# Second mixture of experts: from computing every expert on every token to dispatching rows into capacity buffers by indirect DMA

## The chip, the cores and the metric

The kernel runs on one core of one Trainium2 chip. A core has TensorE (PE: matrix multiplies into PSUM), VectorE (DVE), ScalarE (ACT), GpSimd (POOL) and SyncE (SP, which here only issues DMAs). The engines run their own instruction lists and meet at semaphores. The metric is the device time of one execution in microseconds (us), as the median of several; lower is better. A trace of one execution shows when each instruction ran.

## The reference

Two layers on 8 x 512 = 4096 tokens of width 128. What the change touches is the second layer's mixture and what feeds it.

```python
x = x + s * g                       # end of layer 0: attention output s, gate g = silu(mixture of 64 experts)
xn = layernorm(x)
s = L1_attn(xn)                     # gates from xn, a scan over the 512 tokens of each batch row, a norm
# second mixture: 8 experts, each token picks 2, each expert takes at most 1281 rows
N, K, E = 4096, 2, 8
capacity = int(1.25 * N * K / E) + 1                  # 1281
k_probs, k_idx = top_k(softmax(xf @ router_w.T), K)   # k_probs normalised to sum 1
rank = running count of each expert over the (token, choice) pairs
keep = rank < capacity
buf[flat_e, slot] += xf[token_id] (kept ones)         # [8, 1281, 128]
h = silu(buf @ w1)                                    # w1: [8, 128, 512]
out_buf = h @ w2                                      # w2: [8, 512, 128]
combined = sum over the 2 choices of k_probs * out_buf[flat_e, slot] (kept ones)
g = silu(combined + xn)
x = x + s * g
```

## The kernel before

There are two phases with a barrier between them. `attention_phase` does the first layer's attention in eight stages of four steps (`tau`) each, and stores its results to DRAM. `mixture_phase` does the rest, and is what the change is about.

**Turns and units.** `run_stages` goes over two layers, in each over 8 turns of 512 tokens (`Turn(layer, i, p)`), in each turn over `NQ` = 33 units (layer 0: 64 experts of 64 hidden columns, two to a unit, and a shared expert) or 32 units (layer 1: 8 experts of 512 hidden columns, four units to an expert, `UPC`). Every expert is computed on every token; a gate of zero takes out what was not chosen. A unit is the same chain in both layers, on tiles of 128 x 512:

- PE: three float16 matmuls `m_h` (high and low halves of weight and input), L1510 to L1512
- ACT: Silu in place in PSUM, L1414
- DVE: times the gate row, `m_hid`, L1605
- ACT: high float16 half, `m_hidh`, L1408
- POOL: low half, `m_hidl`, L1375
- PE: three float16 matmuls into `m_y` (`down`), L1490 to L1492, four units later (`LAG`); for layer 1 two further ones per turn add the residual.

**Gates.** The gate rows come from DRAM, spread over partitions by DMAs of SP (`load_gate_pair`, `load_gates`), into a ring of four slots.

**What follows a turn.** While a turn's units run, each engine slips in steps of the turn before (`follow(b, q)` after unit `q`; the tables `PE_AT`, `ACT_AT`, `DVE_AT`, `POOL_AT` say at which). For layer 0 these are: silu of the mixture, times s, transposed, added (`xnew`), stored; layer norm (POOL does the inverse root `rstd`, L1384); transpose; router logits, the two best experts, their shares; the four recurrent gates (float32 matmuls L1559), the scan, a second norm (POOL `crstd`, L1394), the result `s1`; the running rank of each expert ("rank", "cut"), and the gate rows of layer 1 (`cwT`). POOL also splits the normed input in two halves (`m_oh`, `m_ol`, L1389, L1391). For layer 1 only silu, product, transposes and the add follow. The steps of layer 0's last turn run under layer 1's first turn.

**Order.** Each engine's list is fixed by this program; a wait on one engine holds all that is behind it there. The loops for POOL, PE and ACT are in registers (`passes`), those for SP and DVE partly written out.

## Time and profile before

| | |
|---|---|
| median of 3 runs | 1306.46 us (1305.22 to 1307.92) |
| the profiled execution | 1305.83 us, its span in the trace 1304.1 us |
| attention | 0 to about 514 us |
| first mixture's units (layer 0) | about 514 to 942 us |
| second mixture's units (layer 1) and the end | about 942 to 1304 us |
| busy share of the span | PE 92%, DVE 74%, ACT 72%, POOL 63% |

Times in the trace are microseconds from the start of the span. The profiled execution is 1.7 us longer than its span. Durations of one instruction are in ns where marked so; matmuls and activations overlap their neighbours by some tens to 160 ns, so the distance between two starts tells the pace and not the duration.

### The profile page before, as it was taken

What the parts mean: (1) busy time and instruction counts of PE and PEld (TensorE: products, weight loads), DVE (VectorE), ACT (ScalarE), POOL (GpSimd) and SP (SyncE); (2) the same over time, 40 slices, a digit from 0 to 9 for tenths busy, and PEclk for the clock granted to TensorE, in tenths of its full rate; (3) what the DMA queues carried; (4) which work ended last, traced back from release to release, by engine and by line L of the source; (5) the groups of instructions that cost most, each with busy time, mean ns of one, the idle gap of its engine ahead of it and who ended that gap; (6) DMA issues with size and microseconds to landing.
All of it is one profiled execution on the core that took longest, in us unless ns stands there. A gap on an engine that the chain in (4) does not pass through costs nothing.

```text
span 1304.1 us, 21815 instructions
## 1 busy us (share of the span) xinstructions
PE 1199.2 (92%) x5840; PEld 490.8 (38%) x5840; DVE 961.7 (74%) x1802; ACT 935.7 (72%) x1724; POOL 816.9 (63%) x769
## 2 busy tenths in 40 slices
PE   4689998989989996889999899999999999999998
PEld 3123333333333221334444344444444444444443
DVE  4798999989899995567788487777767555555554
ACT  1157676766767775778787577877878888888886
POOL 5423323323332123778888588878878888888887
PEclk9999999999999998999999899999999999999999
DMA  3323040412304037998989789999832333223310
GB/s 71 56 46 70 18 78 13 83 36 51 68 17 73 10 92 218 219 213 185 209 183 190 161 169 197 179 195 197 177 100 62 85 74 81 63 75 72 81 41 9
DMA packets 102171, 137.51 MB, mean 105 GB/s; under 512 B 15546, under 2 KB 54396, under 8 KB 101628
## 3 DMA queue, kind: packets, MB, share of 16 engines
q1 hardware_dynamic: 101532, 136.31, 48.7%
q8 instruction: 36, 0.59, 0.2%
q10 hardware_dynamic: 544, 0.13, 0.2%
q14 instruction: 59, 0.48, 0.1%
HBM read 116.09 MB, written 20.05 MB: 104 GB/s over the span
## 4 chain that ended last, share of the span: by engine, by line
PE 21%; issue 18%; POOL 14%; DMA 3%; ACT 2%; DVE 1%; POOLq 1%; SPq 0%; ACTq 0%; DVEq 0%
POOL m_hidl L1375 13%; DMA p_gates<-t_cw 3%; PE m_h L1510 3%; PE m_y L1490 3%; PE m_h L1512 3%; PE m_h L1511 3%; PE m_y L1492 3%; PE m_y L1491 3%; PE m_m L1559 1%; ACT m_hidh L1408 1%; DVE m_hid L1605 1%; SPq L159 0%; POOL m_rstd L1384 0%; ACT m_h L1414 0%; POOL m_oh L1389 0%
## 5 line engine op out<-in xcount | busy, mean ns | idle before, releaser
L1375 POOL TENSOR_TENSOR m_hidl<-m_hid,m_hidh 128x512 f16<-128x512 f32 x520 | 612.3, 1187 | 135.7 <-ACT m_hidh L1408 101.7
L1605 DVE TENSOR_TENSOR m_hid<-m_h,p_gates 128x512 f32<-128x512 f32 x512 | 348.8, 688 | 243.7 <-ACT m_h L1414 223.8
L707 ACT ACTIVATE a_probs<-a_score 128x512 f32<-128x512 f32 x512 | 293.0, 597 | 123.3 <-PE a_score L788 116.6
L1408 ACT ACTIVATE m_hidh<-m_hid 128x512 f16<-128x512 f32 x520 | 323.0, 621 | 75.9 <-DVE m_hid L1605 73.6
L1414 ACT ACTIVATE m_h<-m_h 128x512 f32<-128x512 f32 x520 | 302.1, 581 | 79.4 <-PE m_h L1512 71.1
L885 DVE TENSOR_REDUCE a_mx<-a_mxps 128x2 f32<-128x1024 f32 x256 | 306.3, 1213 | 38.2 <-PE a_mxps L779 37.5
L800 PE MATMUL a_ops<-a_probs,a_vst 128*32 128x512 f32 x1024 | 136.4, 605 | 0.8 <-ACT a_probs L707 0.8
L583 POOL TENSOR_TENSOR a_crstd<-a_cvareps,a_neghalf 128x1 f32<-128x1 f32 x32 | 18.6, 581 | 157.5 <-DVE a_cvareps L924 143.6
L1490 PE MATMUL m_y<-m_hidh,p_wdh 128*128 128x512 f16 (+1 forms) x264 | 101.0, 383 | 7.2 <-POOL m_hidl L1375 4.2
L788 PE MATMUL a_score<-a_qstack,a_kstack 128*128 128x512 f16 x256 | 96.9, 384 | 8.6 <-ACT a_probs L707 7.0
L788 PE MATMUL a_score<-p_gates,p_raw 128*128 128x512 f16 x256 | 98.8, 387 | 5.9 <-ACT a_probs L707 4.4
L1492 PE MATMUL m_y<-m_hidl,p_wdh 128*128 128x512 f16 (+1 forms) x264 | 100.8, 382 | 0.0
L1491 PE MATMUL m_y<-m_hidh,p_wdl 128*128 128x512 f16 (+1 forms) x264 | 100.8, 382 | 0.0
L779 PE MATMUL a_mxps<-p_raw,p_gates 126*128 126x512 f16 x256 | 83.4, 410 | 18.2 <-DVE a_mx L885 10.5
L1490 PE MATMUL m_y<-m_hidh,m_wdh 128*128 128x512 f16 x256 | 97.1, 379 | 1.3 <-POOL m_hidl L1375 1.3
L1492 PE MATMUL m_y<-m_hidl,m_wdh 128*128 128x512 f16 x256 | 97.0, 379 | 0.0
L1491 PE MATMUL m_y<-m_hidh,m_wdl 128*128 128x512 f16 x256 | 97.0, 379 | 0.0
L575 POOL TENSOR_TENSOR a_ctx<-a_oT,a_rden 128x128 f32<-128x128 f32 x32 | 14.1, 439 | 120.8 <-DVE a_rden L909 120.8
L779 PE MATMUL a_mxps<-a_kstack,a_qstack 126*128 126x512 f16 x256 | 76.5, 380 | 6.5 <-DVE a_mx L885 6.5
L1510 PE MATMUL m_h<-p_xh,p_wuh 128*128 128x512 f16 x132 | 51.9, 394 | 12.2 <-DVE m_hid L1605 9.3
L788 PEld LDWEIGHTS a_score<-a_qstack,a_kstack 128*128 128x128 f16 x256 | 24.1, 97 | 103.1 <-ACT a_probs L707 92.0
L788 PEld LDWEIGHTS a_score<-p_gates,p_raw 128*128 128x128 f16 x256 | 24.9, 97 | 99.6 <-ACT a_probs L707 87.4
(219 smaller groups left out, 1786.9 us busy)
## 6 DMA issues: line engine op xcount, KB each, us to landing
p_gates<-t_cw SPq DMA_DIRECT2D x256, 256.0 KB, 7.2
p_gates<-t_cw SPq DMA_DIRECT2D x32, 512.0 KB, 5.2
t_qparts<-a_qparts SPq DMA_DIRECT2D x32, 128.0 KB
p_raw<-up SPq DMA_DIRECT2D x8, 512.0 KB, 5.5
p_raw<-down SPq DMA_DIRECT2D x8, 512.0 KB, 6.3
m_sT<-t_s SPq DMA_DIRECT2D x16, 256.0 KB, 5.7
a_xin<-x SPq DMA_DIRECT2D x8, 256.0 KB, 3.5
t_kparts<-a_kparts SPq DMA_DIRECT2D x16, 128.0 KB
```

The source lines that it names most:

```text
L707: act.activation(probs[:, kt % 2, g, :], score[:, g % 2, :], ACT.Exp, scale=SCALE / (QS * QS)).then_inc(exp_done, 1)
L779: op = pe.matmul(mxps[:, j % 2, k, :], stack[0][where.p][0:ZROWS, qt, g, at, :], stack[1][where.p][0:ZROWS, :, g, at, :], start=True, stop ...
L788: pe.matmul(score[:, g % 2, :], stack[1][s.p][:, kt, g, tau, :], stack[0][s.p][:, :, g, tau, :], start=True, stop=True).then_inc(score_ful ...
L800: op = pe.matmul(ops[GT * g:GT * g + GT, :], vst[half][:, tau * NG + g, kt, :], probs[:, kt % 2, g, :], start=(kt == 0), stop=(kt == KT - ...
L885: dve.tensor_reduce(mx[ahead % 2][:, j // 2, g:g + 2], mxps[:, j % 2, :, :], AX.X, ALU.max).then_inc(mx_done, 1)
L1375: pool.tensor_tensor(hidl[0:r0, k % r, :], hid[0:r0, k % r, :], hidh[0:r0, k % r, :], ALU.subtract).then_inc(lo_done, 1)
L1408: act.activation(hidh[0:r0, k % r, :], hid[0:r0, k % r, :], ACT.Copy).then_inc(hi_done, 1)
L1414: act.activation(h, h, ACT.Silu, scale=1.0 / WS).then_inc(silu_done, 1)
L1490: pe.matmul(yps[:], wdh[n][0:r0, q, :], hidh[0:r0, r, :], start=(q == 0 and not n), stop=False)
L1491: pe.matmul(yps[:], wdl[n][0:r0, q, :], hidh[0:r0, r, :], start=False, stop=False)
L1492: pe.matmul(yps[:], wdh[n][0:r0, q, :], hidl[0:r0, r, :], start=False, stop=(q == NQ[n] - 1)).then_inc(dn_done, 1)
L1605: dve.tensor_tensor(hid[:, k % r, :], hps[:, k % HBANKS[s.layer], :], gates[:, (q // UPC[s.layer]) % (SLOTS * GROUP), :], ALU.mult).then_i ...
```

## The change

Layer 1 leaves `run_stages`, which now has only the 8 turns of layer 0. The last turn's `follow` steps run by themselves after the units. Instead of `cut` and `cwT`, the step "slots" works out for each token and each of its two choices a row number in a table `slots` in DRAM (8 experts x 1287 places x 144 values: 128 of the normed row, 8 shares, 8 return addresses). POOL sends the rows there by indirect DMA: 8 a turn, 128 rows of 576 bytes each, three of them at q = 27, 29, 31 and five at q = 1, 3, 5, 7, 9 of the turn after. `s1` is transposed back into token rows ("sR"), and xn, s1 and x1 go to DRAM as rows. POOL no longer splits xn. The tables `slots` and `picked` are filled with blanks beforehand, by 16 DMAs of SP in the first eight steps of attention.

A new phase, `expert_phase`, follows behind a barrier: for each expert its 1287 places as 117 partitions x 11 rows, in blocks of 4, 4 and 3 rows, that is 468, 468 and 351 columns; four units to a block, 96 units in all. The DVE's gate multiplication is gone; the low half moves from POOL to DVE. Each block's result is turned back into rows, multiplied by its share, and scattered by POOL with one indirect DMA per row group (88 in all, 117 rows of 512 bytes each) to `picked`. When all have landed, 8 pieces of 512 tokens are read back, two rows per token, added to xn, through Silu, times s, added to x1, stored.

```diff
+CT = 11
+CR = -(-CAPACITY // CT)
+PLACES = CT * CR
+REC = D + 2 * E1
-PE_AT = {"prodT": 6, "xnT": 13, "logits": 14, "f": 15, "i": 16, "z": 17, "o": 18, "cT": 23, "rank": 24,
-         "nT": 30, "cwT": 31}
+PE_AT = {"prodT": 6, "xnT": 13, "logits": 14, "f": 15, "i": 16, "z": 17, "o": 18, "rank": 22, "cT": 23,
+         "nT": 29, "sR": 32}
-POOL_AT = {"rstd": 8, "split": 14, "crstd": 25}
+POOL_AT = {"rstd": 8, "crstd": 25}
+SENT_AT = (27, 29, 31)
+SENT_LATER = (1, 3, 5, 7, 9)
...
@@ attention_phase, SP
+            def blanks_out(k):
+                if k == 0:
+                    sp.wait_ge(pre.blank_ready, 2)
+                into = scratch["slots"][PLACES * k:PLACES * k + PLACES, :].rearrange("(p t) c -> p t c", t=CT)
+                sp.dma_start(into, pre.blank[0:CR, :].unsqueeze(1).broadcast_to([CR, CT, REC])).then_inc(pre.blank_out, 16)
+                into = scratch["picked"][8 * P * k:8 * P * k + 8 * P, :].rearrange("(p t) d -> p t d", t=8)
+                sp.dma_start(into, pre.blank[:, 0:D].unsqueeze(1).broadcast_to([P, 8, D])).then_inc(pre.blank_out, 16)
...
+                if isinstance(s.i, int) and s.i == 0:
+                    blanks_out(TILES * s.p + tau)
@@ mixture_phase, POOL
+            def send(b, j):
+                if j == 0:
+                    pool.wait_ge(placing, b.n("placing", PLACING))
+                    apart(pool)
+                t, k = j // K1, j % K1
+                to = bass.IndirectOffsetOnAxis(slot[b.p][:, TILES * k + t:TILES * k + t + 1], 0)
+                pool.indirect_dma_start(scratch["slots"], to, rec[b.p][:, t, :], None,
+                                        bounds_check=E1 * PLACES - 1, oob_is_err=False).then_inc(sent[b.p], 16)
-                    elif name == "split":
...
@@ mixture_phase, DVE, step "slots" in place of "cut": three element-wise operations on 128x32 or less,
@@ one product 128x64, one reduction, one add, and the two counting operations of before
@@ mixture_phase, end of each engine's list
+            for q in range(NQ[0]):
+                follow(LAST, q)
@@ expert_phase (new)
+BLOCKS = ((0, 4), (4, 4), (8, 3))
+XLAG = 3
+XBANKS = 4
+XRING = 5
+XBUFS = 3
+PIECES = NTOK // (TILES * P)
+PBUFS = 4
...
+        @block.gpsimd
+            for B in range(ALL):
+                e, b, t0, nt = at(B)
+                pool.wait_ge(row_done, B + 1)
+                for t in range(nt):
+                    to = rows_in[e % XBUFS][:, t0 + t, D + E1 + e:D + E1 + e + 1].bitcast(I32)
+                    pool.indirect_dma_start(scratch["picked"], bass.IndirectOffsetOnAxis(to, 0), yrow[b][:, t, :], None,
+                                            bounds_check=K1 * NTOK - 1, oob_is_err=False).then_inc(put[b], 16)
...
+        @block.scalar
+            for g in range(FC * ALL):
+                act.activation(h, h, ACT.Silu, scale=1.0 / WS).then_inc(silu_done, 1)
+                if g: high_part(g - 1)                       # Copy of 128 x n, PSUM to float16
+                if f == 1 and B + 1 < ALL: x_high(B + 1)     # Copy of 128 x n
+                if f == 2 and B: result_out(B - 1)           # Copy of 128 x n
...
+        @block.tensor
+            for g in range(FC * ALL):
+                up(g)                                        # 3 matmuls of n columns
+                if g >= XLAG: down(g - XLAG)                 # 3 matmuls of n columns
+                if f == 0 and B + 1 < ALL: rows_turned(B + 1)  # nt transposes, 117 columns
+                if f == FC - 1 and B: result_turned(B - 1)     # nt transposes
...
+            for n in range(PIECES):
+                pe.wait_ge(pick_in[j], 2 * 16 * (n // PBUFS + 1))
+                pe.matmul(bank, ident[:], pick[1][j], start=True, stop=False)
+                pe.wait_ge(base_done, n + 1)
+                pe.matmul(bank, ident[:], base[n % 2], start=False, stop=True).then_inc(sum_full, 1)
...
+        @block.vector
+            x_low, hidl (scalar_tensor_tensor from PSUM), result_rows (PSUM times share): one each per block, unit, block
```

## Rows read from the trace of the kernel before

**Rows 1.** The page, busy time of each engine over the span.

```profile
PE 1199.2 (92%) x5840; PEld 490.8 (38%) x5840; DVE 961.7 (74%) x1802; ACT 935.7 (72%) x1724; POOL 816.9 (63%) x769
```

**Rows 2.** Windows: start:end, length, busy per engine (instructions), PE clock, DMA share, GB/s.

```profile
0.00:514.00 514.00, 448.51 (x2368) 150.56 (x2368) 441.59 (x826) 321.30 (x603) 170.01 (x217) 0.99 0.27 58
...
888.70:941.90 53.20, 50.66 (x239) 23.33 (x239) 39.14 (x87) 41.23 (x77) 43.04 (x38) 1.00 0.89 189
941.90:995.10 53.20, 50.61 (x240) 23.68 (x239) 38.79 (x87) 40.69 (x76) 42.80 (x37) 1.00 0.34 81
995.10:1037.90 42.80, 42.31 (x199) 19.29 (x198) 25.11 (x36) 36.43 (x68) 37.29 (x33) 1.00 0.33 81
```

**Rows 3.** Timeline of PE, one unit of the second mixture: start, us, what.

```profile
1289.06 0.38 PE L1510 MATMUL m_h<-m_xh,m_wuh 128*128 128x512 f16 x1
...
1290.35 0.38 PE L1510 MATMUL m_h<-m_xh,m_wuh 128*128 128x512 f16 x1
```

**Rows 4.** Groups of instructions, 941.9 to 1295 us (second mixture).

```profile
L1375 POOL TENSOR_TENSOR m_hidl<-m_hid,m_hidh 128x512 f16<-128x512 f32 x258 | 298.8, 1160 | 51.3 <-ACT m_hidh L1408 22.9 <-PE m_y L1492 0.4
```

**Rows 5.** One line's instructions: POOL's shortest group (min/median/max ns).

```profile
L583 POOL TENSOR_TENSOR a_crstd<-a_cvareps,a_neghalf x32: 539/562/941, 85.1 to 506.8; 128x1 f32<-128x1 f32 x32
```

**Rows 6.** DMA issues, two groups: KB each, median us to landing.

```profile
p_raw<-up SPq DMA_DIRECT2D x8, 512.0 KB, 5.5
...
t_s<-p_sT SPq DMA_DIRECT2D x8, 256.0 KB, 2.0
```

**Rows 7.** Timeline of POOL, units 30 to 8 of the next turn.

```profile
942.15 7.09 POOL L1375 TENSOR_TENSOR m_hidl<-m_hid,m_hidh 128x512 f16<-128x512 f32 x6 [0.43 <-ACT m_hidh L1408]
949.60 1.16 POOL L1375 TENSOR_TENSOR m_hidl<-m_hid,m_hidh 128x512 f16<-128x512 f32 x1 [0.36 <-ACT m_hidh L1408]
951.76 2.45 POOL L1375 TENSOR_TENSOR m_hidl<-m_hid,m_hidh 128x512 f16<-128x512 f32 x2 [1.00 <-ACT m_hidh L1408]
954.78 2.45 POOL L1375 TENSOR_TENSOR m_hidl<-m_hid,m_hidh 128x512 f16<-128x512 f32 x2 [0.57 <-ACT m_hidh L1408]
958.59 1.16 POOL L1375 TENSOR_TENSOR m_hidl<-m_hid,m_hidh 128x512 f16<-128x512 f32 x1 [1.36 <-ACT m_hidh L1408]
959.70 1.01 POOL L1384 TENSOR_TENSOR m_rstd<-m_vareps,m_neghalf 128x4 f32<-128x4 f32 x1
```

**Rows 8.** Windows just behind the barrier between attention and mixture.

```profile
514.00:518.00 4.00, 3.76 (x9) 1.20 (x9) 0.25 (x1) 2.21 (x3) 0.18 (x1) 0.50 0.92 295
518.00:524.00 6.00, 5.20 (x24) 2.11 (x24) 3.91 (x7) 5.62 (x12) 4.74 (x5) 1.00 1.06 384
```

**Rows 9.** Timeline of PE: a float32 matmul (two passes); four transposes and the next.

```profile
642.22 1.02 PE L1559 MATMUL m_m<-m_xnT,p_wg 128*128 128x512 f32 x2
...
656.02 0.60 PE L1575 MATMUL m_m<-ident,m_cell 128*128 128x128 f32 x4
656.45 0.38 PE L1510 MATMUL m_h<-p_xh,p_wuh 128*128 128x512 f16 x1
```

**Rows 10.** Timeline of the kernel's end.

```profile
1293.38 0.38 PE L1512 MATMUL m_h<-m_xh,m_wul 128*128 128x512 f16 x1
...
1297.31 0.39 PE L1490 MATMUL m_y<-m_hidh,m_wdh 128*128 128x512 f16 x1 [0.29 <-POOL m_hidl L1375]
...
1300.72 0.69 DVE L1636 TENSOR_TENSOR m_xnew<-m_xres,m_m 128x512 f32<-128x512 f32 x1 [1.23 <-PE m_m L1553]
1301.49 0.38 SPq L1328 DMA_DIRECT2D out<-m_xnew  x1
```

**Rows 11.** Groups on DVE, one turn with follow steps (942 to 996 us).

```profile
L1605 DVE TENSOR_TENSOR m_hid<-m_h,p_gates 128x512 f32<-128x512 f32 x34 | 23.0, 686 | 12.9 <-ACT m_h L1414 12.9
L1659 DVE TENSOR_SCALAR m_xn<-m_xnew,m_mv,m_rstd 128x128 f32<-128x128 f32 x4 | 2.8, 756 | 1.0 <-POOL m_rstd L1384 1.0
```

**Rows 12.** The same normalising in attention, where POOL was idle.

```profile
8.21 1.11 DVE L865 TENSOR_SCALAR a_xn<-a_xin,a_meanvar,a_rstd 128x128 f32<-128x128 f32 x4 [1.22 <-POOL a_rstd L530]
```

**Rows 13.** Timeline of ACT, queued activations at the first mixture's start.

```profile
517.08 1.07 ACT L1414 ACTIVATE m_h<-m_h 128x512 f32<-128x512 f32 x2
```

More of the change, by code:

```diff
@@ L1440, in follow @@
                     if name == "xnT":
-                        if not b.first():
-                            act.wait_ge(split, b.n("two", 0))
                         act.activation(xnT[:], src, ACT.Copy).then_inc(act_rel, 1)
@@ L1470, in _ @@
             run_stages(act, unit, follow)
[L1471 to L1472 removed]
+            high_part(LAST, NQ[0] - 1)
+            for q in range(NQ[0]):
+                follow(LAST, q)
         @block.tensor
@@ L1538, in follow @@
             def follow(b, q):
-                if not b.layer and q == PE_AT["logits"]:
+                if q == PE_AT["logits"]:
                     pe.wait_ge(act_rel, b.n("act_rel", ACT_USES.index("xnT") + 1))
@@ L1583, in follow @@
                     op.then_inc(m_full, 1)
-            pe.wait_ge(cst, 5)
+            pe.wait_ge(cst, 4)
             pe.wait_ge(w_in, 16 * W_LOADS)
             run_stages(pe, unit, follow)
-            last = Turn(1, PASSES - 1, 1)
             for k in range(LAG):
-                down(last, NQ[1] - LAG + k)
-            follow(last, PE_AT["prodT"])
+                down(LAST, NQ[0] - LAG + k)
+            for q in range(NQ[0]):
+                follow(LAST, q)
         @block.vector
@@ L1770, in _ @@
                 dve.memset(priority[:, :, e:e + 1], float(E1 - e)).then_inc(dcst, 1)
-            dve.wait_ge(dcst, 3 + E1)
+            dve.wait_ge(dcst, 2 + E1)
+            dve.wait_ge(cst, 4)
             run_stages(dve, unit, follow, written_out=True)
-            last = Turn(1, PASSES - 1, 1)
-            follow(last, DVE_AT["prod"])
-            follow(last, DVE_AT["xadd"])
+            for q in range(NQ[0]):
+                follow(LAST, q)
+BLOCKS = ((0, 4), (4, 4), (8, 3))
+NB = len(BLOCKS)
```

532 lines of the change are left out of this document (361 added, 171 removed).

## The prediction

> **What bounds the kernel now.** I read the page first: PE is busy 92% of the span [rows 1]. Then the windows by stage [rows 2]. In the second mixture a turn of 32 units takes 42.8 us and PE is busy 42.3 of them: PE is the bound. A unit starts every 1.29 us (1289.06 to 1290.35, [rows 3]), six matmuls at 0.215 us each. POOL is second: 1.16 us for each unit [rows 4]. A turn that also carries follow steps takes 53.2 us, PE busy 50.7, POOL 43.0, ACT 41.2, DVE 39.1 [rows 2]. The second mixture begins at 941.9 us; from there to the end are 362.2 us. These are removed. The rest is the price of what takes their place.
>
> My sum is made against the profiled span, 1304.1 us; 1.7 us lie around it (1305.83), and the median of the runs is 0.6 us above that.
>
> **The one unknown: s.** The trace holds no DMA issued by POOL, so the time s that one indirect DMA holds POOL's queue must be bounded. Below: POOL's shortest instruction is 0.56 us [rows 5]. Above: if POOL were held until the data has landed, the shortest landing is 2.0 us and a usual one 5.5 [rows 6]. The descriptors of 128 rows are small work on all partitions, nearest to POOL's 1.01 us for 128x4 values and 1.16 us for a subtraction of 128x512 [rows 4, 7]. I take s = 1.2 us.
>
> **A. Attention.** Blanking writes 10.1 MB in 16 DMAs over eight steps of some 14 us, 90 GB/s on queues that move 58 GB/s at 0.27 busy [rows 2]; 384 GB/s were moved at 518 us [rows 8]. The next maxima rows are sent a step later, so the transfers are mostly hidden. Uncovered, they would delay eight steps by some 3 us each. With one memset and one iota ahead of the first barrier: +5 us (0 to +25).
>
> **B. The 8 turns.** PE gains four transposes (0.43 us, 656.02 to 656.45, [rows 9]), loses one; ACT gains a copy of 0.5 us; DVE about five small operations, 1 us, at an engine with 14 us idle. About 0.4 us a turn, 3 in all. The sends stand between units 27 and 9 of the next turn. Behind each of them on POOL waits the next `m_hidl`, and PE's `down` waits for that. In this stretch POOL idles 0.43 + 0.36 + 1.00 + 0.57 + 1.36 + about 0.5 = 4.2 us [rows 7]. The last unit of the kernel shows how long the chain is: its last up matmul starts at 1293.38 (at the pace of 0.215 it is through at 1293.6), and `down`, waiting for the low half alone, starts at 1297.31 [rows 10], 3.7 us later. In the stream PE comes to it after four units, 5.2 us: 1.5 us of cover. So a turn loses 8s - 5.7 us, 3.9 us at s = 1.2, in 6.4 such stretches: 25 us. After unit 9 POOL catches up (its split, 2.5 us, is gone). Gate rows arrive beside 0.6 MB more a turn, 11 GB/s upon 189 [rows 2]; since 384 was possible [rows 8], I add 3 for it. B = 3 + 25 + 3 = +31.
>
> Row and rule: four normalising operations took 2.8 us beside a busy POOL [rows 11] and 1.1 us beside an idle one [rows 12], so DVE and POOL do hold one another up. The Trainium skill ("SBUF — State Buffer", "SBUF: two separate sides") says that some DVE operations lock GpSimd out, and that descriptors of its DMAs then wait. By it a send that meets `prod` (q = 4) would take about 1 us longer, some 7 us in all; the new phase's DVE operations mostly read PSUM and would not do it.
>
> **C. The last turn's follow, now bare.** I count from 941.9, where the next unit would have started, 0.65 us (a `down`) after the last up matmul. The old end has that last matmul through at 1293.6 and `xnew` at 1301.4 [rows 10]: 7.8 us, so 7.1 from that point. Of DVE's 38.8 us in a turn with follow 23.0 are the gate products [rows 2, 11], so about 15 are follow work; 2.4 are in the 7.1, 1.7 go since normalising is quick alone. Serial with it are transposes and copies (1.2 + 0.6), logits (1.1), the recurrent gates (4 of at most 1.0, [rows 9]) and two inverse roots of POOL (2.0, [rows 7]), some in parallel. I walk the chain thus: row statistics and norm to 11.2 us, transposes, copy and logits to 14.6, first choice to 16, second after the f gate to 18.4, gates and scan to 22.4, shares 23.5, rank 24.1, slots 26.2, second statistics 28, `crstd` 29.1. It stands ahead of the sends in POOL's list. Then 8 sends, 8s = 9.6, and 2.5 for landing plus 0.8 for waits. C = 32.4 + 8s = 42. The other end (s1, nT, sR) is done earlier, at 35.
>
> **D. Barrier and first rows.** Barrier 1 us; 741 KB land in about 6.5 (512 KB take 5.5, [rows 6]); transposes, two copies 2.5. D = 10.
>
> **E. Experts.** PE, by columns at 0.215 us for 512: a matmul of 468 takes 0.197, of 351 0.148. A block of four row groups: 24 x 0.197 + 8 transposes at 0.11 [rows 9] = 5.6 us; of three: 24 x 0.148 + 6 x 0.11 = 4.2. 16 x 5.6 + 8 x 4.2 = 123 us. ACT has ten activations a block at 0.49 us for 512 [rows 13], that is 4.5 to 4.9 us; DVE six of about 0.6. PE bounds as long as a send takes under 1.4 us (four in 5.6); beyond it POOL does, at 88s. PE has idled before: behind the barrier of before, where it had idled too, the granted clock was 0.50, the 1.2 GHz level, up to 518 [rows 8], so +2; run-in and run-out +3. E = max(123, 88s) + 5. It replaces 256 units by 96 narrower ones: this is where the gain comes from.
>
> **F. The end.** Last result: copy, transposes, product 2.1, three sends 3s = 3.6, landing and waits 3 us. Then 8 pieces: 4.2 MB in and 2.1 MB out, 21 us at 300 GB/s (295 at 514 us, [rows 8]); but piece n + 4 waits for piece n, and one passage is landing 5.5 + POOL and DVE and PE and ACT 4.7 us, the next pieces behind it at 2.2. So 10.2 for the first, 21 for the fifth, 28 for the eighth, and 2.6 to land. F = 35.4 + 3s = 39.
>
> Sum: 941.9 + 5 + 31 + 42 + 10 + 128 + 39 = 1197 us span, 1199 measured. In general, with B = 6 + 6.4 (8s - 5.7), T(s) = 1001 + 62.2s + max(123, 88s), for s over 0.71.
>
> **The rivals.**
> *POOL light.* s of 0.71 or less: no loss in the turns, all sends hidden but the last 11. T = 1037.5 + 11s + 123, about 1168. For it: POOL's 0.56 us row. Against: 128 addresses must be handled one by one.
> *POOL becomes the bound but the change still pays.* s from 1.4 to 1.95: T = 1211 to 1294, say 1250. For it: DVE and POOL hold one another up [rows 11, 12]; stretch B has only 5.7 us of room.
> *The other side: each send holds POOL till its data is acknowledged.* s of 2.03 is where T reaches 1306; at 2.5 it gives 1001 + 155.5 + 220 = 1376. For it: the shortest landing is 2.0 us [rows 6], and 64 + 88 sends sit in POOL's in-order list. Against: SP's queue issues its DMAs in 0.38 us [rows 10], long before they land. The Trainium skill ("DMA: Bandwidth & Descriptors", "Anatomy of one DMA — SWDGE (gpsimd) path") gives a fixed 2.0 us for a GpSimd DMA and puts most of it to the write's receipt and not to the queue; if it held the queue the sum would be 1301, no gain to speak of.
> *The gain is hidden.* PE is at its bound in the removed part [rows 2, 3], so removing its work can't be hidden; I give it nothing of its own.
>
> **How the numbers follow.** Forecast (s 0.8 to 1.4) 0.52; POOL light 0.14; POOL bound but faster 0.22; other side 0.10; the last 0.02 for T within 0.2% of 1306, which is about what a measurement of this kernel can tell from no change. Faster 0.87, same 0.02, slower 0.11. The time is that of the forecast, 1199. The range runs from 1150 (s near 0.56, attention and the end 12 us better) to 1285 (s = 1.9), leaving out some 2 in 10. The likeliest case alone has 1170 to 1225.
>
> **What would show it.** The trace after should have POOL's indirect DMAs with their length s; turns of 57 us with waits of `m_y` for `m_hidl` around unit 27 to 9; a stretch of about 42 us with PE nearly idle near 970 us; blocks of 5.6 and 4.2 us with PE near 95% and POOL under it; an end of about 39 us. If `m_y` or the yrow products wait for POOL throughout, s is over 1.4. What would make it wrong: s, above all; attention slower by more than 10 us through the blanks; the bare chain C, which I only walked.

## The result, and the profile after

The changed kernel takes 1262.85 us (median of 4 runs, 1261.98 to 1263.2) against 1306.1 us for the kernel before in the same comparison: ratio 0.967, 95% interval 0.966 to 0.968. The gain is 43 us; the forecast was 107. The profiled execution took 1263.2 us, its span is 1261.5 us, where the sum had given 1197. Of all executions in this document one, of the later variant x_pe_nops, took 2055.8 us where the others took about 1262; its time and its trace are left out.

The page of the changed kernel: busy time of each engine (beside [rows 1]), and the two groups of sends of POOL, with their count, busy us, mean ns, and the idle time before them.

```profile
PE 1033.9 (82%) x5064; PEld 421.3 (33%) x5064; DVE 899.2 (71%) x1737; ACT 766.1 (61%) x1452; POOL 666.2 (53%) x658
...
L1899 POOL DMA_INDIRECT t_picked<-e_yrow,e_rows x88 | 87.0, 989 | 95.0 <-DVE e_yrow L2033 72.0
...
L1390 POOL DMA_INDIRECT t_slots<-m_rec,m_slot x64 | 65.7, 1026 | 12.2 <-issue 11.4
```

A send keeps POOL busy for 1.0 us, and sends that stand in a row start 1.27 to 1.30 us apart. The one unknown of the forecast, s = 1.2, was right within 0.1 us. PE is busy for 82% of the span where it was 92%: time was lost in waiting.

Windows of the changed kernel, columns as in [rows 2]: attention; one turn; from the last unit of the turns to the first `up` of the second mixture; the second mixture; the end.

```profile
0.00:514.00 514.00, 448.32 (x2368) 150.06 (x2368) 441.07 (x815) 320.35 (x600) 169.06 (x214) 1.00 0.35 78
882.80:944.90 62.10, 51.85 (x241) 22.94 (x239) 45.48 (x92) 41.61 (x76) 48.83 (x44) 1.00 0.70 171
1003.90:1060.80 56.90, 20.52 (x71) 10.28 (x69) 16.96 (x64) 9.28 (x17) 21.84 (x22) 0.60 0.24 73
1060.80:1214.80 154.00, 133.76 (x726) 73.19 (x727) 79.46 (x138) 104.98 (x234) 76.16 (x77) 0.97 0.29 92
1214.80:1261.50 46.70, 22.16 (x55) 8.56 (x53) 13.89 (x22) 7.11 (x15) 21.81 (x19) 0.81 0.43 145
```

Attention is as long as before, though it now moves 78 GB/s and not 58. The turn is the first surprise: 62.1 us against 53.2 in [rows 2], and PE works only 1.2 us more in it (51.85 against 50.66). So PE waits 7.7 us more in each turn. In the second mixture PE is busy 133.8 of 154 us. Divided at the places where the forecast divides it, the span is:

| part | forecast | measured | from where to where |
|---|---|---|---|
| A, attention | 5 | 2.3 | the first Silu of the mixture stands at 519.38 us, before at 517.08 [rows 13] |
| B, the turns | 31 | 60.8 | the last unit of the turns stands at 1005.0, before at 941.9 |
| C and D, bare steps, barrier, first rows | 52 | 55.8 | 1005.0 to the first `up` at 1060.8 |
| E, experts | 128 | 157.3 | 1060.8 to the last `down`, through at 1218.1 |
| F, the end | 39 | 43.4 | 1218.1 to 1261.5 |
| sum | 255 | 319.6 | |

Two terms hold 59 of the missing 65 us: B, twice as large as forecast, and E.

### The profile page after: what moved, and what is told of

Read it like the earlier page. It is cut to its first block and busy times, and to the rows that moved or that the text cites. A ratio compares the mean times of both kernels' runs of the same rounds, so it can differ in the third digit from the quotient of the medians.

```text
span 1261.5 us, 18713 instructions
## 1 busy us (share of the span) xinstructions
PE 1033.9 (82%) x5064; PEld 421.3 (33%) x5064; DVE 899.2 (71%) x1737; ACT 766.1 (61%) x1452; POOL 666.2 (53%) x658
## 5 line engine op out<-in xcount | busy, mean ns | idle before, releaser
L1380 POOL TENSOR_TENSOR m_hidl<-m_hid,m_hidh 128x512 f16<-128x512 f32 (+1 forms) x264 | 316.9, 1216 | 102.5 <-ACT m_hidh L1425 97.5
L1608 DVE TENSOR_TENSOR m_hid<-m_h,p_gates 128x512 f32<-128x512 f32 x256 | 172.4, 686 | 117.0 <-ACT m_h L1431 88.8
L1425 ACT ACTIVATE m_hidh<-m_hid 128x512 f16<-128x512 f32 (+1 forms) x264 | 163.9, 621 | 109.0 <-DVE m_hid L1608 107.3
L1431 ACT ACTIVATE m_h<-m_h 128x512 f32<-128x512 f32 (+1 forms) x264 | 153.1, 580 | 41.8 <-PE m_h L1519 32.6
L1899 POOL DMA_INDIRECT t_picked<-e_yrow,e_rows x88 | 87.0, 989 | 95.0 <-DVE e_yrow L2033 72.0
L1500 PE MATMUL m_y<-m_hidh,p_wdh 128*128 128x512 f16 (+1 forms) x264 | 101.6, 385 | 13.5 <-POOL m_hidl L1380 12.4
L2043 DVE SCALAR_TENSOR_TENSOR e_hidl<-e_h,e_hidh 128x468 f16<-128x468 f32 (+1 forms) x96 | 58.0, 605 | 75.6 <-ACT e_hidh L1917 63.7
L1936 ACT ACTIVATE e_h<-e_h 128x468 f32<-128x468 f32 (+1 forms) x96 | 51.1, 532 | 43.3 <-PE e_h L1981 29.0
L1390 POOL DMA_INDIRECT t_slots<-m_rec,m_slot x64 | 65.7, 1026 | 12.2 <-issue 11.4
L1517 PE MATMUL m_h<-p_xh,p_wuh 128*128 128x512 f16 x132 | 51.7, 392 | 19.9 <-DVE m_hid L1608 17.4
```

Of the source, the lines that this page charges most:

```text
L1380: pool.tensor_tensor(hidl[0:r0, k % r, :], hid[0:r0, k % r, :], hidh[0:r0, k % r, :], ALU.subtract).then_inc(lo_done, 1)
L1425: act.activation(hidh[0:r0, k % r, :], hid[0:r0, k % r, :], ACT.Copy).then_inc(hi_done, 1)
L1431: act.activation(h, h, ACT.Silu, scale=1.0 / WS).then_inc(silu_done, 1)
L1500: pe.matmul(yps[:], wdh[n][0:r0, q, :], hidh[0:r0, r, :], start=(q == 0), stop=False)
L1608: dve.tensor_tensor(hid[:, k % r, :], hps[:, k % HBANKS[s.layer], :], gates[:, (q // UPC[s.layer]) % (SLOTS * GROUP), :], ALU.mult).then_i ...
```

## The experiments

Eighteen further runs were made, in five groups, each group on one chip beside the kernel before, whose median was 1304.8 to 1309.5 us. The tables on the turns are worked out from the timelines: the distance from one unit's Silu to the next one's, as the median of five turns (the third to the seventh), and the times of the first and of the last unit's Silu. The turns of the changed kernel stand unchanged in four further variants (after_again, x_no_sends, x_spread, no_sends_2): with them, first to last unit is 482.6 to 486.6 us, so a difference under 4 us over the eight turns says little.

### What the turns lose

**t_no_sends**: the turns without their sends.

```diff
-                if q in SENT_AT:
-                    send(b, SENT_AT.index(q))
...
-                if q in SENT_LATER:
-                    send(b, len(SENT_AT) + SENT_LATER.index(q))
+                return
...
-                            dve.wait_ge(sent[b.p], b.half("sent", 0))
```

> The 64 sends of the turns and the waits for them are left out, so the table of slots stays blank and the second mixture's 88 sends have addresses out of bounds: they are issued but move nothing. Turns take 62.2 us in the changed kernel (from the fourth on, 52.7 before). Theory 1 (the sends hold up POOL's low halves and stretch VectorE's operations on SBUF): turns fall to 53.5 to 55 us, some 55 us less at the start of the second phase. Theory 2 (the loss sits in TensorE's new waits and the longer slots step): turns stay at 59 us or more. In the expert phase: if the late updates of TensorE's semaphores come from the sends' data and receipts, an expert falls from 19.7 to under 17 us; if from POOL's issuing alone or from the order of the program, it stays at 19.7.

Measured: 1204.1 us (1204.0 to 1204.6). From the first unit to the last are 458.4 us and not 485.9: the sends cost 27.5 us of the turns (24 to 25 against x_no_sends and x_spread, which ran on the same chip with the turns unchanged). But a turn is still 58.0 us long, over the first theory's range and under the second's: each holds for a part.

**t_back_no_sends** and **t_no_slots** divide what is left. The first puts the follow steps where they stood before the change, the second leaves the arithmetic of the slots out; neither sends.

```diff
-PE_AT = {..., "o": 18, "rank": 22, "cT": 23, "nT": 29, "sR": 32}
+PE_AT = {..., "o": 18, "cT": 23, "rank": 24, "nT": 30, "sR": 32}
-DVE_AT = {..., "share": 21, "slots": 24, "cstats": 24, "caggr": 25, "cnorm": 27, "s1": 30}
+DVE_AT = {..., "share": 21, "cstats": 24, "caggr": 25, "cnorm": 27, "slots": 28, "s1": 31}
```

```diff
-                        dve.tensor_scalar(over[:], ranks, ...)
-                        dve.scalar_tensor_tensor(rec[b.p][:, :, D + E1:].bitcast(I32), chosen[1], ...)
-                        dve.tensor_scalar(start_of[:], priors[:], ...)
-                        dve.tensor_tensor(ranked, ranks, over[:], ALU.add)
-                        dve.tensor_tensor(placed, ranked, picks[:], ALU.mult)
-                        dve.tensor_reduce(place[:], placed, AX.X, ALU.add)
-                        dve.tensor_tensor(slot[b.p][:], place[:], start_of[:], ALU.add)
+                        dve.tensor_copy(start_of[:, 0:1, :], bank(b, "rank")[:, 0:TILES].unsqueeze(1))
```

> No turn sends (and so a blank table, as in the first variant without them), and the follow steps of TensorE and VectorE at the places they had before the change. Turns took 57.9 us without sends at the changed places and 52.7 before the change. If the changed places are the cause, turns take 53.5 to 55 us. If the larger VectorE work is (slots step, its operations on SBUF), they stay at 57 to 58.

> No turn sends and no slots arithmetic either (one copy stands in its place; the counting stays), at the changed places. If the slots step, 3 us of VectorE ahead of the cell statistics, is the cause, turns fall from 57.9 to 55 or 56 us, at units 26 and 29; the wait at unit 22 for the rank's input stays (1.4 us). If it hides, they stay at 57.9.

Measured: 1208.0 us (1206.0 to 1208.9) and 1209.7 us (1209.3 to 1211.6) in all, both with the experts of 19.7 us that the last part of this section is about. The turns are the point here:

| us after unit | 3 | 6 | 9 | 12 | 22 | 26 | 29 | 30 | 32 | turn | first unit | last unit | between them |
|---|---|---|---|---|---|---|---|---|---|---|---|---|---|
| before | 1.5 | 1.7 | 2.2 | 4.2 | 2.0 | 1.3 | 2.2 | 1.7 | 1.0 | 52.8 | 517.1 | 942.1 | 425.1 |
| after | 2.0 | 3.2 | 3.8 | 5.1 | 3.4 | 3.4 | 3.4 | 1.0 | 1.8 | 62.2 | 519.4 | 1005.2 | 485.9 |
| t_no_sends | 1.5 | 1.7 | 2.2 | 4.2 | 3.4 | 3.4 | 3.4 | 1.0 | 1.8 | 58.0 | 519.7 | 978.0 | 458.4 |
| t_no_slots | 1.5 | 1.7 | 2.2 | 4.2 | 3.4 | 1.3 | 2.9 | 1.0 | 1.8 | 55.8 | 519.5 | 965.3 | 445.8 |
| t_back_no_sends | 1.5 | 1.7 | 2.2 | 4.2 | 2.0 | 1.3 | 2.0 | 3.5 | 2.3 | 55.7 | 520.8 | 963.3 | 442.5 |

Between the first unit and the last, 33.3 us have nothing to do with sends (458.4 against 425.1). Of these the slots step where it stands costs 12.6 (458.4 to 445.8; a turn of 55.8 us lies in the range expected), mostly at unit 26: it is queued ahead of the cell statistics and of the next units' `m_hid` on DVE. Taking all steps back to their old units gives 15.9 (to 442.5; a turn of 55.7 us is 0.7 over its range, but far from the 57 to 58 of the other case): the wait of the rank at unit 22 goes (1.4 us a turn), and the slots step, now at 28, moves its loss to unit 30 (3.5 us against 1.7 before), where the `m_hid` behind it comes late. With the steps back, 17.5 us remain (442.5 against 425.1). By the turns in the table it is 2.9 us a turn: 1.8 at unit 30 and 1.3 at unit 32, where the new transposes of `s1` stand. The waits of PE in a turn of the changed kernel (882.8 to 944.9; us in total, times, longest) name them: L1517 is a unit's first matmul, L1555 the transpose of `prod`, L1559 the transpose of xn, L1568 the rank, L1585 the nT step.

```profile
PE m_h L1517 <- DVE m_hid L1608: 1.9, 2, 1.0
PE m_m L1559 <- DVE m_rec L1658: 1.8, 1, 1.8
PE m_m L1568 <- issue: 1.8, 1, 1.8
PE m_m L1585 <- DVE m_cn L1703: 1.6, 1, 1.6
PE m_y L1500 <- POOL m_hidl L1380: 1.5, 4, 0.6
...
PE m_m L1555 <- DVE m_prod L1629: 0.9, 1, 0.9
```

### How a send costs a turn its time

The forecast had the low halves behind the sends late for `down`. That wait is the row of L1500 above, 1.5 us, only 0.9 more than in t_no_sends (0.6). The waits for DVE grow by 2.6: for `m_hid` from 1.0 to 1.9, for `m_rec` from 1.0 to 1.8, for `prod` from nothing to 0.9. The units that grow with the sends are 3, 6, 9 and 12. At unit 6 PE waits for `prod`. The timeline of the changed kernel there, DVE and POOL:

```profile
889.91 3.35 DVE L1629 TENSOR_TENSOR m_prod<-m_gT,m_sT 128x512 f32<-128x512 f32 x1
...
889.40 0.99 POOL L1390 DMA_INDIRECT t_slots<-m_rec,m_slot  x1 [0.17 <-issue]
890.41 2.29 POOL L1380 TENSOR_TENSOR m_hidl<-m_hid,m_hidh 128x512 f16<-128x512 f32 x2
892.86 1.26 POOL L1390 DMA_INDIRECT t_slots<-m_rec,m_slot  x1 [0.17 <-issue]
```

The same operation in t_no_sends, and `m_vareps`, which takes 2.6 us in the changed kernel:

```profile
870.61 1.68 DVE L1624 TENSOR_TENSOR m_prod<-m_gT,m_sT 128x512 f32<-128x512 f32 x1
...
876.74 1.06 DVE L1644 TENSOR_SCALAR m_vareps<-m_mv 128x4 f32<-128x4 f32 x1
```

In the bare steps of the last turn, where POOL has sends but no low halves to work on, it takes 0.69 us (below, at 1013.37). So `m_prod` needs about 0.7 us of its own. In the changed kernel it starts at 889.91, and is through at 893.26, 0.56 us after the two low halves of POOL end at 892.70. Behind a send POOL has low halves waiting, and works them off without a pause. `m_vareps` shows the same in the changed kernel:

```profile
897.32 2.60 DVE L1649 TENSOR_SCALAR m_vareps<-m_mv 128x4 f32<-128x4 f32 x1
```

It ends at 899.92; POOL works on two low halves from 897.61 to 899.88. So these two operations of DVE, which read SBUF alone, wait until such a run ends. The Trainium skill ("SBUF — State Buffer", "SBUF: two separate sides") calls the port that DVE and GpSimd share an exclusive lock, taken for the whole instruction by a GpSimd operation or by a DVE operation that runs in a two-port mode or has two SBUF inputs. By that rule the row of `m_prod`, with its two inputs, agrees in kind; that DVE stands back for several instructions in a row is what the row adds. `m_vareps` has a single input and waits too; whether it runs in the two-port mode no trace shows. The send at 892.86, beside the end of `m_prod`, takes 1.26 us and not 0.99.

**t_late_sends** moves the sends to units where POOL idles.

```diff
-SENT_AT = (27, 29, 31)
-SENT_LATER = (1, 3, 5, 7, 9)
+SENT_AT = ()
+SENT_LATER = (12, 13, 14, 16, 17, 18, 20, 22)
```

> Same work; a turn's eight sends move from after units 27, 29, 31, 1, 3, 5, 7, 9 to after units 12, 13, 14, 16, 17, 18, 20, 22 of the next turn, where the float32 matmuls stretch the units and POOL idles. Theory 1 (sends collide with VectorE's SBUF operations of units 4 to 11 and with the low halves of dense units): turns fall from 62.2 to 57 to 59 us, the kernel by 20 to 35 us. Theory 2 (waits in the follow steps alone): turns within 1 us of 62.2.

Measured: 1230.1 us (1229.1 to 1233.1), ratio 0.942 (0.940 to 0.943). The units 3 to 12 are as without sends (1.5, 1.7, 2.2, 4.2 us), so it is the sends there that cost the 4 us. But a turn still takes 61.0 us, over the 57 to 59 expected: unit 26 now takes 1.9 us more (5.3 against 3.4), for which the sends at 20 and 22 are the likely cause. The last unit stands at 995.2, so 10 of the 33 us come from the turns. Most of the others came from the second mixture, where nothing was changed; of that below.

**t_back_late** and **t_back_dense** put the follow steps back too. The first keeps this list of sends; the second sends after each of the units 11 to 18.

> As the variant with late sends, and TensorE's and VectorE's follow steps go back to where the kernel before had them: cT 23, rank 24, nT 30; slots at 28 where the cut was, s1 at 31, sR stays at 32. Without sends the turns still took 57.9 us against 52.7, and per unit the loss sat at units 22 (1.4), 24 to 26 (2.5), 29 (1.2) and 32 (0.9). If TensorE's waits for the rank's input and the slots step queued ahead of the cell statistics are its cause, turns fall from 60.4 to 56 to 57.5 us, the kernel to 1200 to 1210. If the longer VectorE work itself is, the loss only moves and the turns stay over 59.

> As the one before with the eight sends after each of the units 11 to 18, ahead of the steps on the rank and the slots. In the late variant units 22 to 28 took 2.9 us more than without sends, beside its sends at 20 and 22; if these collide with VectorE's operations on SBUF there, this one is 1.5 to 2.5 us a turn faster than the one before (some 15 us in all). If one send per unit overloads POOL (1.16 + 1.3 us per unit), it is slower.

Measured: 1242.6 us (1241.5 to 1244.4) and 1241.8 us (1240.4 to 1243.6); turns of 60.8 and 60.3 us, last unit at 987.4 and 986.6. From the first unit to the last they take 468.7 and 467.3 us; without sends it had been 442.5 with the steps in this order, so the sends cost 25 to 26 us in either list. In t_back_dense POOL works nearly without a gap over units 12 to 24, and units 20 to 23 take 4.1 us more than without sends. Both expectations missed: a turn of t_back_late is over the 56 to 57.5 us of its range (its other case, over 59, came true), and the two lists are equally good. Both kernels are also 12 us slower than t_late_sends, although their turns are shorter, because an expert takes 19.7 us in them and 16.95 in t_late_sends; of that too below.

**best_back** and **best_after** place the sends where the timelines showed POOL idle, with the steps back and with the steps of the changed kernel; both have the spread of the next part.

```diff
+SENT_LATER = (12, 12, 14, 15, 16, 18, 30, 32)
```

> Old places of the follow steps, a turn's sends after units 12 (two), 14, 15, 16, 18, 30 and 32, where POOL was seen idle, and the spread sends in the second mixture. In the dense variant POOL ran without a gap from unit 12 to 24 and its low halves held TensorE for 2.5 us a turn at units 20 to 23. If that is all the sends cost, turns fall from 60.1 to 57.5 to 58.5 us and the kernel, with experts of 16.9 us, to 1203 to 1213.

> The same list of sends and the spread on the follow steps' places of the changed kernel, whose turns took 57.9 us without any sends. If the sends fit where POOL idles, turns take 57.9 to 58.8 us and the kernel 1204 to 1214; if they still collide with the steps at units 22 to 32, some 60.5 and 1225.

Measured: 1223.5 us (1222.4 to 1227.4) and 1259.9 us (1259.6 to 1260.6); turns of 59.7 and 64.8 us. Neither expectation held: the first's turns are 1.2 us longer than its range, the second is worse than all before it, with 6.7 us after unit 22. Its timeline there, DVE and POOL:

```profile
932.26 3.01 DVE L1750 TENSOR_TENSOR m_selh<-m_picks 128x32 bf16<-128x32 f32 x1
...
930.09 1.73 POOL L1390 DMA_INDIRECT t_slots<-m_rec,m_slot  x1 [0.17 <-issue]
931.85 3.38 POOL L1380 TENSOR_TENSOR m_hidl<-m_hid,m_hidh 128x512 f16<-128x512 f32 x3
```

`m_selh` is a sum over 128x32 values, 0.18 us long in the changed kernel. Here it begins under a run of three low halves, and ends at 935.27, 0.04 us behind the run (935.23). The rank's matmul waits for it.

**best2_spread** tests this by itself: the first choice is written once more, to PSUM, so that `m_selh` reads one operand from there. It is a DVE operation more per turn.

```diff
+                        dve.tensor_tensor(first_choice, rated[0], wide(prior[0]), ALU.is_equal)
...
-                        dve.tensor_tensor(selh[:], chosen[0], chosen[1], ALU.add)
+                        dve.tensor_tensor(selh[:], first_choice, chosen[1], ALU.add)
```

> Best variant so far (1223.5 us) with one more VectorE operation: the first choice is written to PSUM once more, so that the operation that makes the rank's input reads one operand from PSUM. It had taken up to 3.0 us instead of 0.2 where POOL ran without a gap. If an operand in PSUM frees it from POOL, units 22 to 24 take 1 to 2.5 us less a turn and the kernel 1206 to 1217 us; if it waits for POOL whatever it reads, the kernel stays at 1223 to 1225.

Measured: 1221.9 us (1219.7 to 1225.1), ratio 0.932 (0.929 to 0.935), over the 1206 to 1217 expected. With best_back, whose times overlap its own, it is the fastest version that does the whole work. The group of DVE in one turn, best_back above and best2_spread below it (in best_back six of the eight turns have 3.02 us, in best2_spread all eight have 0.19):

```profile
L1750 DVE TENSOR_TENSOR m_selh<-m_picks 128x32 bf16<-128x32 f32 x1 | 3.0, 3024 | 0.0
```

```profile
L1753 DVE TENSOR_TENSOR m_selh<-m_m,m_picks 128x32 bf16<-128x32 f32 x1 | 0.2, 192 | 0.1
```

POOL was as busy there as before; a turn of best2_spread, DVE and POOL:

```profile
906.06 0.19 DVE L1753 TENSOR_TENSOR m_selh<-m_m,m_picks 128x32 bf16<-128x32 f32 x1
...
905.44 5.62 POOL L1381 TENSOR_TENSOR m_hidl<-m_hid,m_hidh 128x512 f16<-128x512 f32 x5
```

So 3.02 us became 0.19 by the place of one operand, and unit 23 takes 2.8 us instead of 4.3; the turn 58.7 instead of 59.7, the last unit stands at 979.1 instead of 983.7. The kernel gained 1.6 us of these 4.6, which is within the spread of its runs; its experts were slower (18.2 us against 17.7).

### What the second mixture loses

From the first `up` of one expert to that of the next are 19.7 us in the changed kernel; the forecast's blocks make 15.4 (5.6 + 5.6 + 4.2). **x_no_sends** takes the 88 sends out, **x_spread** spaces them.

```diff
-                for t in range(nt):
-                    pool.indirect_dma_start(scratch["picked"], ...).then_inc(put[b], 16)
```

```diff
                 for t in range(nt):
+                    if FC * (B + 2) + t + 1 <= FC * ALL:
+                        pool.wait_ge(lo_done, FC * (B + 2) + t + 1)
```

> The 88 sends of the second mixture are left out (and the waits for them), so the end reads blank rows. Theory S (the sends delay TensorE's semaphore updates): no update comes over 0.4 us late, an expert takes 15.4 to 16.8 us instead of 19.7, the phase is 23 to 34 us shorter, and the end another 10 us shorter. Theory P (order of the program: the narrow block with three transposes, the in-order list of ScalarE): the expert stays within 0.5 us of 19.7 and only the end shrinks, by some 10 us.

> Same work; each of the 88 sends waits for one more unit's low half, so that POOL sends one per unit and never eight in a row at 1.3 us. If long runs of sends back to back are what delays TensorE's updates, an expert falls from 19.7 us to 16 to 18. If any send does it, or the order of the program, it stays within 0.5 us of 19.7 or rises.

Measured: 1227.5 us (1226.5 to 1231.6) and 1242.3 us (1240.2 to 1244.6). Experts take 16.95 us in both, and also in t_no_sends and t_late_sends, whose 88 sends are issued as in the changed kernel. So a send does not cost the experts anything as such. (16.95 is over the 15.4 to 16.8 expected of x_no_sends, and both runs seemed to bear out that the sends make the difference; the kernels below take that back.) Without sends the end is shorter: 34.2 us from the last `up`, against 46.7.

The 16.95 us are PE's own time. The timeline of t_late_sends, PE alone, from the last unit of a block over the transposes to the next:

```profile
1142.76 0.36 PE L1979 MATMUL e_h<-e_xh,p_wuh 128*128 128x468 f16 x1
...
1143.97 0.69 PE L1968 MATMUL e_o<-ident,e_yT 128*117 128x128 f32 x4
1144.64 0.32 PE L1979 MATMUL e_h<-e_xh,p_wuh 128*128 128x351 f16 x1
...
1145.69 0.56 PE L1959 MATMUL e_x<-ident,e_rows 117*128 117x117 f32 x4
1146.10 0.31 PE L1979 MATMUL e_h<-e_xh,p_wuh 128*128 128x351 f16 x1
```

The matmuls run at the forecast's pace (six of 468 columns in 1142.76 to 1143.97, 1.2 us). Four transposes of the rows take 0.41 us, as forecast (0.43), but four of a result 0.67. Behind the narrow block PE waits some 0.4 us ahead of them, and they take 0.9 us there. The eleven of a result take 2.6 us an expert with that wait where I had 1.2, which is most of the 1.55 us between 15.4 and 16.95: 12 us in all.

What makes 19.7 of 16.95 is stranger. The changed kernel, third expert, PE, ACT and POOL:

```profile
1102.00 0.31 PE L1992 MATMUL e_y<-e_hidl,p_wdh 128*128 128x351 f16 x1
...
1102.55 0.36 PE L1981 MATMUL e_h<-e_xh,p_wul 128*128 128x468 f16 x1
...
1102.68 0.57 ACT L1917 ACTIVATE e_hidh<-e_h 128x468 f16<-128x468 f32 x1
...
1104.99 0.46 ACT L1929 ACTIVATE e_yT<-e_y 128x351 f32<-128x351 f32 x1 [1.74 <-PE e_y L1992]
1105.50 0.59 PE L1968 MATMUL e_o<-ident,e_yT 128*117 128x128 f32 x3 [2.00 <-ACT e_yT L1929]
...
1107.12 0.55 ACT L1936 ACTIVATE e_h<-e_h 128x468 f32<-128x468 f32 x1 [1.67 <-PE e_h L1981]
```

ACT's `e_yT` waits for the semaphore of the `down` at 1102.00, which is through at 1102.31 (a second condition, a transpose of the block before the last, was met long ago). It starts at 1104.99, after 1.74 us of idling, and PE idles for 2.00 us since it waits for ACT: both wait at once, for something that the trace has as done. The next Silu (1107.12) reads what the `up` at 1102.55 wrote. In t_late_sends the same step of an expert follows at once:

```profile
1119.41 0.31 PE L1992 MATMUL e_y<-e_hidl,p_wdh 128*128 128x351 f16 x1
...
1120.53 0.48 ACT L1929 ACTIVATE e_yT<-e_y 128x351 f32<-128x351 f32 x1
1120.87 0.60 ACT L1936 ACTIVATE e_h<-e_h 128x468 f32<-128x468 f32 x1
```

The trace also records updates of semaphores. I compared those of PE with the ends of its matmuls: in the kernel before none of some 2,100 comes over 0.3 us late. In the second mixture of the changed kernel 52 of some 200 do, by up to 4 us, in one stretch of 2 to 5 us in each expert from the second on; at its end five or six updates come within 0.3 us. Besides, 38 of the 239 updates that were due there have no record. Records are missing for the other engines too, 51 of 239 updates of ACT and 41 of 143 of DVE, though none of theirs that is recorded is late.

**after_again** and **x_pe_nops** asked whether this belongs to the program.

```diff
+            for k in range(24):
+                pe.nop(nofuse=True)
             rows_turned(0)
```

> The changed kernel once more, unchanged, beside the three below. If the late updates of TensorE's semaphores belong to this program, they come again: experts of 19.7 us, 1263 us in all. If they belonged to the chip or the day, experts take the 16.9 us that four variants with the same expert code showed, and the kernel some 1242 us.

> Same work; 24 empty instructions on TensorE ahead of the expert loop, while it waits for the first rows anyway, so that the loop's instructions lie at other addresses and nothing else changes. If the place of the instructions matters for the late updates, experts fall from 19.7 to 16.9 us and the kernel to some 1242 us; if the timing of sends against units does, it stays at 1263.

Measured: 1262.7 us (1261.4 to 1266.1), with 53 late updates; and 1261.7 us (1259.0 to 1265.2, ratio 0.966) with the empty instructions, of which only the times are used. It comes again, and the place of PE's instructions is not it.

Then three attempts at the sends in flight: **dense_spread** (t_back_dense with the spread), **dense_landed** (POOL waits ahead of each block's sends until those of the block before have landed) and **best2_landed** (best2 with that wait ahead of the second block only, in place of the spread).

```diff
                 pool.wait_ge(row_done, B + 1)
+                if B:
+                    pool.wait_ge(put[(B - 1) % NB], put_by((B - 1) % NB, (B - 1) // NB + 1))
```

```diff
                 pool.wait_ge(row_done, B + 1)
+                if b == 1:
+                    pool.wait_ge(put[0], put_by(0, e + 1))
```

> The variant with sends after units 11 to 18 and the old places of the follow steps (1241.8 us, experts of 19.7 us with late updates), with the 88 sends of the second mixture spread over the units. If spreading them is what keeps TensorE's updates on time, experts take 16.9 us as in the first spread variant and the kernel some 1221 us. If the late updates come and go with something else in the program, it may stay at 1242.

> The same base; POOL waits, ahead of a block's sends, until those of the block before have landed, which breaks the run of eight into four and four with a gap of about 1 us and leaves at most four sends in flight. If the number of sends in flight sets off the late updates, experts take 16.9 us and the kernel some 1222; if not, they stay at 19.7 and it stays at 1242.

> The same, and in the second mixture, instead of the spread, POOL waits ahead of the second block's sends until the first block's four have landed. If more than four sends in flight delay TensorE's updates, experts take 16.9 to 17.2 us (spread: 17.0 to 18.2) and the kernel is 3 to 8 us faster than best2_spread; if the number in flight does not matter, experts take up to 19.7 us and it is 5 to 15 us slower.

Measured: 1227.8 us (1226.2 to 1229.7), 1250.3 us (1248.9 to 1251.7), 1236.6 us (1234.6 to 1237.5). The spread helped dense_spread only in part: 15 late updates and experts of 17.5 us, between its two cases. In dense_landed nearly all recorded updates are on time (3 late, but 57 of 238 have no record), and the experts take 16.95 us until POOL, with 11 sends and three landings an expert (11 x 1.3 + 3 x 2.3 = 21 us), becomes the bound: 20 and 21 us for the last two, and the last send 32 us behind the last `up`. But best2_landed, in which the first block's four have landed before the second block's begin, has 54 late updates: the run of eight sends in the wide blocks is not what is needed for them. The second case of its expectation came true: it is 15 us slower than best2_spread.

Last, **late_sends_2** and **no_sends_2**: the only traces without late updates had all come from one chip.

> The late-sends variant once more, unchanged (1230.1 us, experts of 16.9 us, no update late). If the late updates belong to the chip, and this is not the chip of the first call, it now has them: experts of 19.7 us, the kernel at some 1249 us. If they belong to the program, experts take 16.9 us again and the kernel 1230.

> The variant without the 88 sends once more, unchanged (1227.5 us, experts of 16.9 us). If the other shows late updates and this one does not, they need the sends: experts 16.9 us, 1228 us in all. If this one has them too, they have nothing to do with the sends, and experts take about 19.7 us, the kernel some 1247.

Measured: 1229.9 us (1228.9 to 1232.3) and 1230.5 us (1229.3 to 1232.7), experts of 16.94 us, no update late, on the chip on which dense_spread, best_back and best_after had shown them. For these two it is the program and not the chip. t_no_sends and x_spread have run only on that first chip, on which nothing was late, so for them the two are not separated.

| kernel | late updates | updates of PE without a record, of 239 | us an expert, 2nd to 7th |
|---|---|---|---|
| t_late_sends, late_sends_2, t_no_sends, x_no_sends, no_sends_2, x_spread | 0 | 0 | 16.95 |
| after, after_again, t_back_late, t_back_dense, best2_landed | 52 to 54 | 38 to 55 | 19.7 to 19.9 |
| t_back_no_sends, t_no_slots (sends without a valid address) | 50 to 51 | 30 to 33 | 19.7 to 19.8 |
| dense_spread, best_back, best_after, best2_spread | 15 to 45 | 42 to 53 | 17.5 to 18.2 |

The third column divides the traces as sharply as the second: no record is missing in the six without late updates, of PE, ACT or DVE, and 18 to 29% of those of the three together are missing in every other one. Lateness and lost records go together here; which leads to which, no run shows.

## Why the prediction was wrong, step by step

**s.** Right: 1.27 to 1.30 us from send to send, 1.2 forecast. With it fell the rivals "POOL light" and "each send holds POOL till its data is acknowledged": sends follow one another at 1.3 us, while the landing of the last one takes from 1228.32 to about 1230.7, when the first read behind it is issued. The Trainium skill ("DMA: Bandwidth & Descriptors", "Anatomy of one DMA — SWDGE (gpsimd) path") puts most of its 2.0 us to the receipt; by that rule the trace agrees, with a landing of 2.4 us beside a pace of 1.3. POOL did not become the bound either.

**A.** Mis-sized by 3 us: 2.3 instead of 5, a miss no larger than the spread of the first unit's time over kernels with the same attention (518.7 to 521.6).

**B, the step that failed.** "PE gains four transposes [...], loses one; ACT gains a copy [...]; DVE about five small operations, 1 us, at an engine with 14 us idle. About 0.4 us a turn, 3 in all." These 3 us, with another 3 for gate rows that arrive beside more traffic, were 33.3 us without any send. I costed the new work by its length against the engine's idle time, and the moved steps (`rank` 24 to 22, `nT` 30 to 29, the slots at 24 where the cut had been at 28) at nothing. Each engine's list is in order: 3 us of DVE work ahead of the cell statistics hold `m_hid`, and a transposing step put a unit earlier makes PE wait for its input. t_no_slots and t_back_no_sends price these at 12.6 and 15.9 us, which overlap. The work itself was larger too: without sends DVE is busy for 41.5 us of a turn (863.9 to 921.9 in t_no_sends), 2.4 us more than the 39.1 before. What the gate rows cost was not tried. That the new step `sR` causes the 1.3 us a turn at unit 32 was not tried by itself.

The sends' term, 25 us, measured 24 to 28. The size was right by luck, since the mechanism was not. The 8s - 5.7 us of late low halves are 0.9 us of waiting in a turn; 2.6 of the 4.2 us a turn are PE's waits for DVE, held by the runs of low halves that a send leaves behind. I had the rows for it [rows 11, 12], but put the price of one microsecond on the send that meets `prod`, not on `prod`, and left even that out of the sum.

**C and D.** Right within 4 us. The bare chain of the changed kernel, DVE, POOL, SP and PE:

```profile
1013.37 0.69 DVE L1629 TENSOR_TENSOR m_prod<-m_gT,m_sT 128x512 f32<-128x512 f32 x1 [6.84 <-ACT m_gT L1444]
...
1036.11 1.04 POOL L1406 TENSOR_TENSOR m_crstd<-m_cvareps,m_neghalf 128x4 f32<-128x4 f32 x1 [15.99 <-DVE m_cvareps L1697]
...
1037.35 1.03 POOL L1390 DMA_INDIRECT t_slots<-m_rec,m_slot  x1 [0.20 <-issue]
...
1046.31 0.97 POOL L1390 DMA_INDIRECT t_slots<-m_rec,m_slot  x1 [0.30 <-issue]
...
1052.83 1.17 SPq L1861 DMA_DIRECT2D e_rows<-t_slots  x3
...
1058.42 1.04 PE L1959 MATMUL e_x<-ident,e_rows 117*128 117x117 f32 x4 [15.84 <-DMA e_rows<-t_slots]
```

The walk had `crstd` at 29.1 us from the last unit; it starts 31.1 us from it. The eight sends take 9.9 us, and 5.5 us lie between the last one's end and the first load.

**E, the second large miss.** 157.3 instead of 128 us. Without late updates it is 138 (late_sends_2, between the same points), so some 20 us go with the late updates. The other 10 are 12 from transposes of a result, which take PE 0.17 us each and not 0.11, and from the wait behind the narrow block, less some 3 of the 5 us that I had allowed for start and end. Nothing in the trace of before could show the late updates. That the sends would be hidden under PE there was right.

**F.** 43.4 instead of 39: POOL still has eight sends to start behind the last `down`, and PE's float32 matmuls start at the lower clock level: from 1234 to 1240 us the granted clock is 0.50, the 1.2 GHz level, behind 16 us in which PE was busy for 0.6.

```profile
1228.32 0.99 POOL L1899 DMA_INDIRECT t_picked<-e_yrow,e_rows  x1 [0.30 <-issue]
...
1230.76 3.67 SPq L1878 DMA_DIRECT2D p_gates<-t_picked  x8
...
1234.03 2.07 PE L2013 MATMUL e_h<-p_gates,ident 128*128 128x512 f32 x2 [14.77 <-DMA p_gates<-t_picked]
1235.89 1.91 PE L2015 MATMUL e_h<-p_raw,ident 128*128 128x512 f32 x2
...
1242.28 1.02 PE L2013 MATMUL e_h<-p_gates,ident 128*128 128x512 f32 x2
```

**Open.** What sets off the late updates. Shown: the changed kernel had them in two executions and two other programs had none on either of two chips; they come on at least three chips, and need neither the sends' data nor the eight sends in a row of the wide blocks (four of the five kernels with the spread still had 15 to 45). With the spread they were shorter, and with the full wait for landings (dense_landed) nearly gone. Whether some smaller number in flight matters stays open. The one program without the 88 sends had none, but some with all of them had none either, so that they need sends is not shown. Programs with the same list for PE had them and had them not. Records are missing in just the traces that have them, which would fit a path of records that is full. Every execution here has its span and granted clock on record, the timed ones too, and none was timed without them. So a rival stands untested: that the recording itself delays PE, and that an execution without it would lack these 20 us. The Trainium skill ("NOTIFIC — the notification-queue block", "Overflow: three behaviours, one of which stalls the engine") describes a back-pressure of such records onto the engines; whether that happens here no run shows.

## What to carry to other kernels

New work on an engine with idle time is free only if nothing is queued behind it that somebody waits for: price each inserted or moved step by the next instruction on its engine, not by the engine's idle share. Where POOL works in long runs, a small DVE operation with all operands in SBUF may take as long as the run; read one operand from PSUM, or leave POOL gaps there. And where a phase is off its plan, compare identical code in two variants' traces before explaining it by the program's structure.

## What was not expected of the hardware

- A DVE sum of 128x32 values took 3.02 us (best_back) beside three POOL subtractions of 128x512 in a row, and 0.19 us with one operand in PSUM (best2_spread), beside five.
- TensorE's semaphore updates came up to 4.4 us behind the matmuls' ends, in 12 of 18 traces that can be read, from the same TensorE list that had none late in others; in the same 12 traces, and in no other, updates of PE, ACT and DVE lack their records in the second mixture.
- An indirect DMA of 128 rows of 576 bytes, or 117 rows of 512, held POOL for 0.97 to 1.0 us, 1.73 us in some turns of best_back and best2_spread, and up to 1.98 us beside a DVE operation of 2.06 us on SBUF (dense_spread, at 648.55); in a row they start 1.27 to 1.30 us apart.
